# Feed-forward columns in five chunks of 128, and the last 42 of value and gate in one product

## The chip, the cores and the metric

The kernel runs on one NeuronCore of a Trainium2 chip. TensorE (PE; its weight loads are listed as PEld) multiplies, VectorE (DVE), ScalarE (ACT) and GpSimd (POOL) work element by element, SyncE (SP) issues most DMAs. The metric is the device time of one execution in microseconds (us), the median of several. All data are float32.

## What is computed

The reference is a stack: a chunked retention layer, two layers of local attention with a gated feed-forward, a latent attention, and a mixture of experts. The change touches the feed-forward of the two local-attention layers:

```python
DIM = 256
DEPTH = 2
HID = int(DIM * 4 * 2 / 3)          # 682
...
h = shift_token(x)
mu = h.mean(-1, keepdims=True)
var = h.var(-1, keepdims=True)
h = (h - mu) / jnp.sqrt(var + 1e-05) * lg + lb
h = h @ w1 + b1                      # w1: 256 x 1364
a, g = jnp.split(h, 2, axis=-1)      # value a and gate g, 682 columns each
h = a * jax.nn.gelu(g, approximate=False)
x = x + h @ w2 + b2
```

## The kernel before

The 4096 tokens go through in 8 pieces of 512. With two layers there are 16 items, k = 0 to 15, and the loop over `stages()` runs one stage for each: its feed-forward, beside the attention of the next item (`s.ahead`), and in stages 0 to 7 the retention layer (`s.ret`), in stages 8 to 15 the latent attention of a finished piece (`s.lat`, `s.behind`). Stage 15 is the last and has no next item. After it come 71 tiles of the experts. Each engine has its own program and the order in it is written out by hand; the engines meet at semaphores: `mmA` and `mmD` count finished products of PE, `outA` (ACT), `outS` and `outD` (DVE) count results that were read out of PSUM.

PSUM is two rings of four banks. Ring A (`pA`) is read mainly by ACT, ring D (`pD`) by DVE. `ring_a_jobs()` and `ring_d_jobs()` list the products in order; `bank_ring` gives each one or two banks (two start at an even bank, so that one may be left empty ahead of them) and works out which reader has to be done before PE may write there.

The feed-forward of one item, transposed (columns of `w1` on the partitions, the 512 tokens along the row), runs in `NHC` = 6 chunks of `HCH` = 120 inner columns, the last of 82:

- PE, `up_projection(b, c)`: the gate ("g", ring A), then the value ("a", ring D), each 2 matmuls of 512 columns over 256 inputs (`project`, L703). The profile records each float32 matmul twice, so that a product is 4 records.
- ACT, `gelu(b, c)` (L1252): the gate with its bias out of ring A to `gl`.
- DVE, `gate_up(b, c)` (L1674): (value + bias) x gelu to `hT[c]`. Before the last chunk a memset (L1673) puts ones below its 82 rows, and the row of ones carries the bias `b2`.
- PE, `down_projection(b)` (L703 from `hT` and `w2` to `pD`): 24 matmuls, behind a wait for the last `gate_up`.

After the last chunk PE does, in stages 0 to 8, the first two score products of the next item, S0 and S1 (`local_scores`, L753), and then the down-projection. In stages 9 to 14 two groups of transposes of the latent attention stand ahead of S0 (`turn_attention`, L714), which ACT copies to `curT` (L1278) after the last gelu. In stage 15 a `latent_values` product (L870) stands there, and no scores. ACT goes on with the exponentials (L1209), for which it first loads another table; DVE with the row maxima of S0 (L1634).

Of the kernel before, what the change touches and what calls it, by code (L numbers as in the profile page):

```python
# [26 lines left out]
HCH = 120  # L27
NHC = 6
HSZ = [min(HCH, HID - HCH * c) for c in range(NHC)]

# [61 lines left out]
def ring_a_jobs():  # L92
# [3 lines left out]
    for s in stages():  # L96
# [22 lines left out]
        for c in range(NHC):  # L119
            if s.here:  # L120
                j += [("g", k, c)]
            if s.ahead and c == 0:
                j += [("qkT", k + 1, 1)]
            if s.last and c == 1:
                j += [("av", b - 1, 2)]
            if s.behind and c == (5 if s.last else 3):
                j += [("av", b - 1, 3)]
            if s.ret and 1 <= c < 5:
                j += [("rT", k, c - 1)]
            if s.behind and c == 5 and not s.last:  # L130
                j += [("attnT", b - 1, 0), ("attnT", b - 1, 1)]
            if s.ahead and c == 3:
                j += [("qkT", k + 1, 2)]
            if s.ahead and c == 4:
                j += [("qkT", k + 1, 3)]
# [124 lines left out]
def stream_layers(nc, I, x_d, S, out_d):  # L260
# [17 lines left out]
    with ctx:  # L278
# [7 lines left out]
        by_layer = (("wqkv", [P, DC, 3 * INNER]), ("wo", [P, 4, D]), ("ln", [P, 2, DC]), ("w1", [P, DC, 2 * HID]),  # L286
# [196 lines left out]
        norm_x = sem("norm_x")  # L483
        fin_silu = sem("fin_silu")
# [41 lines left out]
        def _(sp):  # L526
# [23 lines left out]
            for s in stages():  # L550
# [34 lines left out]
                if k == B - 1:  # L585
                    sp.wait_ge(outA, doneA["g", k, NHC - 1])
# [75 lines left out]
        def _(pe):  # L662
# [126 lines left out]
            def up_projection(b, c):  # L789
                n = HSZ[c]  # L790
                if c == 0:
                    pe.wait_ge(outA, doneA["zT", b, 1])
                ps = slotA("g", b, c)
                project(ps[0:n, 0:T], lambda k: W["w1"][:, k, HID + c * HCH:HID + c * HCH + n], lambda k: zT[:, k, :], DC).then_inc(mmA, 1)
                ps = slotD("a", b, c)
                project(ps[0:n, 0:T], lambda k: W["w1"][:, k, c * HCH:c * HCH + n], lambda k: zT[:, k, :], DC).then_inc(mmD, 1)
# [364 lines left out]
        def _(act):  # L1161
# [85 lines left out]
            def gelu(b, c):  # L1247
                n = HSZ[c]
                ps = takeA("g", b, c)
                if b > 0 or c >= 2:  # L1250
                    act.wait_ge(outD, doneD["a", b, c - 2] if c >= 2 else doneD["a", b - 1, NHC - 1])
                nc.scalar.activation(gl_of(b)[c % 2][0:n], ps[0:n, 0:T], ACT.Gelu, bias=W["b1"][0:n, 1, c:c + 1]).then_inc(outA, 1)  # L1252
# [312 lines left out]
        def _(dve):  # L1565
# [102 lines left out]
            def gate_up(b, c):  # L1668
                n = HSZ[c]
                ps = take("a", b, c)  # L1670
                dve.wait_ge(outA, doneA["g", b, c])
                if c == NHC - 1:
                    step(nc.vector.memset(hT_of(b)[NHC - 1][64:HCH], 1.0))  # L1673
# [473 lines left out]
def arrange(a):  # L2147
# [13 lines left out]
    r["w_w1"] = np.stack([ch(w) for w in a["L0_ffn_w1"]], 1)  # L2161
    b1 = np.zeros((HCH, DEPTH, 2, NHC), np.float32)
    w2 = np.zeros((HCH, DEPTH, NHC, D), np.float32)
    for l in range(DEPTH):
        for c in range(NHC):
            n = HSZ[c]
            for i in range(2):
                b1[0:n, l, i, c] = a["L0_ffn_b1"][l, i * HID + c * HCH:i * HID + c * HCH + n]
# [46 lines left out]
```

## Time and profile before

| | |
|---|---|
| median of 3 runs | 3048.02 us (3040.27 to 3054.22) |
| the profiled execution | 3047.79 us, its span 3045.9 us |
| PE busy | 2770.7 us, 91% of the span |
| DVE, ACT, POOL busy | 53%, 40%, 35% |
| the chain that ended last | PE 73%, DVE 12%, issue 4%, DMA 4%, POOL 3%, ACT 3% |
| mean granted TensorE clock | 0.963 of full speed |

A timeline row is: start, us, engine, line, operation, what is written from what, shapes, number of records, and in brackets how long the engine was idle before it and who released it. A group row gives, after the number of records, busy us and mean ns of one record, and the idle time in front. PE's records overlap: in a row of matmuls the next starts before the modelled end of the one ahead, so that spacing is read from starts. A stage lasts about 137 us up to stage 6 and 157 to 163 us from stage 9.

### The profile page before, as it was taken

What the parts mean: (1) busy time and instruction counts of PE and PEld (TensorE: products, weight loads), DVE (VectorE), ACT (ScalarE), POOL (GpSimd) and SP (SyncE); (2) the same over time, 40 slices, a digit from 0 to 9 for tenths busy, and PEclk for the clock granted to TensorE, in tenths of its full rate; (3) what the DMA queues carried; (4) which work ended last, traced back from release to release, by engine and by line L of the source; (5) the groups of instructions that cost most, each with busy time, mean ns of one, the idle gap of its engine ahead of it and who ended that gap; (6) DMA issues with size and microseconds to landing.
All of it is one profiled execution on the core that took longest, in us unless ns stands there. A gap on an engine that the chain in (4) does not pass through costs nothing.

```text
span 3045.9 us, 42333 instructions
## 1 busy us (share of the span) xinstructions
PE 2770.7 (91%) x15646; PEld 1863.9 (61%) x15646; DVE 1627.9 (53%) x3890; ACT 1213.3 (40%) x2265; POOL 1077.0 (35%) x767
## 2 busy tenths in 40 slices
PE   6999999999999899999989898999988899999992
PEld 3565656556565656555555555555554488999992
DVE  6656566575656456676676768585754520000003
ACT  4444444535344444444444544444543232222221
POOL 5423243343423233353444535353532321111113
PEclk8999999999999999999999999999998799999996
DMA  3000000000001011001010101010000367999886
GB/s 134 11 23 17 25 28 25 15 25 15 25 22 46 25 40 59 20 5 49 4 49 4 49 4 42 11 39 15 29 15 31 132 233 268 343 357 344 326 325 206
DMA packets 85767, 261.72 MB, mean 86 GB/s; under 512 B 10653, under 2 KB 49901, under 8 KB 66877
## 3 DMA queue, kind: packets, MB, share of 16 engines
q1 hardware_dynamic: 79084, 241.25, 21.9%
q0 software_dynamic: 6480, 17.77, 1.5%
q8 instruction: 128, 2.10, 0.3%
q14 instruction: 75, 0.61, 0.1%
HBM read 210.68 MB, written 44.11 MB: 84 GB/s over the span
## 4 chain that ended last, share of the span: by engine, by line
PE 73%; DVE 12%; issue 4%; DMA 4%; POOL 3%; ACT 3%; SPq 1%; POOLq 0%; DVEq 0%; ACTq 0%
PE s_pD L703 20%; PE s_pA L703 17%; PE s_pD L1155 7%; PE s_pA L1140 6%; PE s_pD L860 3%; PE s_pA L753 3%; PE s_pD L775 3%; PE s_pA L762 3%; DMA s_w_w<-rows_s 3%; DVE s_pairs L1735 2%; PE s_pA L742 2%; DVE s_qk L1634 2%; PE s_pA L870 2%; ACT s_qk L1209 1%; PE s_pD L941 1%
## 5 line engine op out<-in xcount | busy, mean ns | idle before, releaser
L1456 POOL TENSOR_TENSOR s_qk<-s_qk,s_rrec 128x1024 f32<-128x1024 f32 (+1 forms) x128 | 215.7, 1685 | 578.0 <-DVE s_rrec L1640 577.9
L1209 ACT ACTIVATE s_qk<-s_qk,s_mx 128x256 f32<-128x256 f32 (+1 forms) x512 | 239.9, 469 | 341.0 <-DVE s_mx L1634 340.3
L703 PE MATMUL s_pA<-s_w_wqkv,s_curT 128*128 128x512 f32 x768 | 354.3, 601 | 5.6 <-ACT s_curT L1185 3.7
L703 PEld LDWEIGHTS s_pA<-s_w_wqkv,s_curT 128*128 128x128 f32 x768 | 142.4, 191 | 176.6 <-issue 163.1
L1735 DVE TENSOR_SCALAR s_pairs<-s_pD 128x1024 f32<-128x1024 f32 (+1 forms) x192 | 194.4, 1038 | 103.9 <-PE s_pD L860 101.1
L2086 DVE COPY s_w_wo<-s_pD 128x256 f32<-128x256 f32 x71 | 30.0, 423 | 409.6 <-PE s_pD L1126 409.6
L1555 POOL DMA_INDIRECT acc_s<-s_w_w,s_sq x71 | 68.3, 962 | 458.9 <-ACT s_w_w L1397 451.6
L1450 POOL TENSOR_TENSOR s_rinv<-s_ssq,s_half 128x16 f32<-128x16 f32 x64 | 207.5, 3242 | 5.1
L860 PE MATMUL s_pD<-s_mixer 32*128 32x512 f32 (+3 forms) x1024 | 186.4, 477 | 23.6 <-DVE s_pairs L1735 18.5
L1446 POOL TENSOR_TENSOR s_qk<-s_qk,s_rot 128x1024 f32<-128x1024 f32 x64 | 150.5, 2351 | 135.5 <-DVE s_qk L1617 135.4
L703 PE MATMUL s_pA<-s_zT,s_w_w 128*120 128x512 f32 (+1 forms) x384 | 186.7, 609 | 1.1 <-ACT s_zT L1225 1.1
L1634 DVE CUSTOM_DVE_ANT_0 s_qk<-s_pA,s_maskw 128x256 f32<-128x256 f32 (+1 forms) x512 | 167.9, 385 | 31.2 <-PE s_pA L753 30.7
L1270 ACT ACTIVATE s_pairs<-s_pairs 128x2560 f32<-128x2560 f32 x64 | 149.7, 2338 | 87.3 <-DVE s_pairs L1735 87.2
L703 PE MATMUL s_pD<-s_zT,s_w_w 128*120 128x512 f32 (+1 forms) x384 | 181.7, 596 | 0.0
L860 PEld LDWEIGHTS s_pD<-s_mixer 32*128 32x128 f32 x1024 | 91.6, 193 | 130.6 <-issue 84.4
L1414 POOL TENSOR_TENSOR s_rs<-s_ve,s_half 128x4 f32<-128x4 f32 x40 | 41.1, 1026 | 363.9 <-DVE s_ve L1596 363.9
L762 PE MATMUL s_pA<-s_ident,s_qk 128*128 128x128 f32 x896 | 129.8, 287 | 40.3 <-issue 23.7
L753 PE MATMUL s_pA<-s_qkT 64*128 64x256 f32 (+1 forms) x1024 | 131.7, 380 | 29.9 <-DVE s_mx L1634 14.7
L1191 ACT COPY s_qk<-s_pA 128x1024 f32<-128x1024 f32 x64 | 64.6, 1010 | 217.2 <-PE s_pA L703 217.2
L762 PEld LDWEIGHTS s_pA<-s_ident,s_qk 128*128 128x128 f32 x896 | 99.2, 144 | 83.8 <-issue 58.1
L703 PEld LDWEIGHTS s_pD<-s_zT,s_w_w 128*120 128x120 f32 (+1 forms) x384 | 69.1, 180 | 98.6 <-issue 97.9
L1397 ACT ACTIVATE s_w_w<-s_pD,s_w_w 128x256 f32<-128x256 f32 x71 | 33.6, 473 | 236.8 <-PE s_pD L1155 236.8
(276 smaller groups left out, 5922.9 us busy)
## 6 DMA issues: line engine op xcount, KB each, us to landing
s_qkT<-in_m_w SPq DMA_DIRECT2D x48, 1024.0 KB, 5.2
s_v_tm<-in_m_w SPq DMA_DIRECT2D x24, 1024.0 KB
s_rot<-in_m_w SPq DMA_DIRECT2D x24, 1024.0 KB, 5.1
s_w_wqkv<-in_m_w SPq DMA_DIRECT2D x23, 1024.0 KB
s_qk<-in_m_w SPq DMA_DIRECT2D x23, 1024.0 KB, 6.1
s_w_w<-rows_s SPq DMA_DIRECT2D x71, 129.0 KB
s_cur<-in_x SPq DMA_DIRECT2D x8, 512.0 KB, 3.5
xn_s<-s_cur SPq DMA_DIRECT2D x8, 512.0 KB, 2.8
```

The lines of the kernel that those rows point to most:

```text
L703: last = nc.tensor.matmul(out, lhs(c), rhs(c), start=(c == 0), stop=(c == n - 1))
L753: last = nc.tensor.matmul(ps[:, place(i) * 256 + lo * P:(place(i) + 1) * 256], qkT[r, h // 2, tile_cols(t)], qkT[r, 4 + h // 2, (t - 1 + l ...
L762: last = nc.tensor.transpose(ps[:, (2 * i + k) * P:(2 * i + k + 1) * P], prob[w % 3][:, i * 256 + k * P:i * 256 + (k + 1) * P], ident[:])
L860: last = nc.tensor.matmul(ps[:, 512 * i + col:512 * i + col + T - kt * P], KT[rows, g % 2, tile_cols(kt)], QT[rows, g % 2, kt * P:T], star ...
L1140: last = nc.tensor.matmul(m_ph[u % 2][:, f * P:(f + 1) * P], m_w1[u % NW][:, c * F + f * P:c * F + (f + 1) * P], m_xT[:, u % 2, c * P:(c + ...
L1155: last = nc.tensor.matmul(m_py(w), m_hT[w % 2][:, f * P:(f + 1) * P], m_w2[w % NW][:, f * D:(f + 1) * D], start=(f == 0), stop=(f == FC - 1))
L1209: last = nc.scalar.activation(pi, pi, ACT.Exp, scale=-1.0, bias=mx[:, u, i:i + 1], accum_out=rsum[:, u, i:i + 1])
L1446: nc.gpsimd.tensor_tensor(qk[:, t, :], qk[:, t, :], rot[:, t % 2, :], ALU.add)
L1450: nc.gpsimd.tensor_tensor(rinv[:, t, :], ssq[:, t, :], half[:], ALU.pow).then_inc(rinv_rdy, 1)
L1456: nc.gpsimd.tensor_tensor(pi, pi, rrec[:, u, :].unsqueeze(2).broadcast_to((P, 4, 256 - lo)), ALU.mult).then_inc(p_rdy, 1)
L1634: last = nc.vector.tensor_tensor_reduce(out=prob[u % 3][:, h], in0=ps[:, h], in1=maskw[:, lo:256], scale=-1.0, scalar=3e38, op0=ALU.add, o ...
L1735: nc.vector.tensor_scalar(Pl[:, w % SLOTS, :, ROUND_AT[r]:ROUND_AT[r] + ROUND_N[r]], ps[:, :, 0:ROUND_N[r]], 80.0, -80.0, ALU.min, ALU.max ...
```

## The change

`HCH` becomes 128: five chunks of 128 inner columns and a last one of 42. The columns of `w1` are laid out in the order in which they are used: for each chunk its values, then its gates, and for the last chunk 42 values, 22 columns of zeros and 42 gates (`LAST_G` = 64). The last chunk is one product of 106 rows in ring D. ACT reads its gelu from rows 64 to 105 of that bank and counts it on a semaphore of its own, `last_gelu`; DVE waits for that, sets the ones in rows 32 to 63 of `hT[5]`, and reads the values from rows 0 to 41 of the same bank. The last gate leaves ring A's list.

```diff
-HCH = 120
+HCH = 128
 NHC = 6
 HSZ = [min(HCH, HID - HCH * c) for c in range(NHC)]
+LAST_G = 64
+UPW = 2 * HCH * (NHC - 1) + LAST_G + HSZ[-1]
...
         for c in range(NHC):
-            if s.here:
+            if s.here and c < NHC - 1:
                 j += [("g", k, c)]
...
                 if k == B - 1:
-                    sp.wait_ge(outA, doneA["g", k, NHC - 1])
+                    sp.wait_ge(outA, doneA["g", k, NHC - 2])
...
             def up_projection(b, c):
-                n = HSZ[c]
                 if c == 0:
                     pe.wait_ge(outA, doneA["zT", b, 1])
-                ps = slotA("g", b, c)
-                project(ps[0:n, 0:T], lambda k: W["w1"][:, k, HID + c * HCH:HID + c * HCH + n], lambda k: zT[:, k, :], DC).then_inc(mmA, 1)
+                at = 2 * HCH * c
+                if c < NHC - 1:
+                    ps = slotA("g", b, c)
+                    project(ps, lambda k: W["w1"][:, k, at + HCH:at + 2 * HCH], lambda k: zT[:, k, :], DC).then_inc(mmA, 1)
+                n = HCH if c < NHC - 1 else LAST_G + HSZ[c]
                 ps = slotD("a", b, c)
-                project(ps[0:n, 0:T], lambda k: W["w1"][:, k, c * HCH:c * HCH + n], lambda k: zT[:, k, :], DC).then_inc(mmD, 1)
+                project(ps[0:n, 0:T], lambda k: W["w1"][:, k, at:at + n], lambda k: zT[:, k, :], DC).then_inc(mmD, 1)
...
             def gelu(b, c):
                 n = HSZ[c]
-                ps = takeA("g", b, c)
+                at = 0 if c < NHC - 1 else LAST_G
+                if c < NHC - 1:
+                    ps = takeA("g", b, c)
+                else:
+                    act.wait_ge(mmD, DJ["a", b, c] + 1)
+                    ps = pD[:, colsD[DJ["a", b, c]]]
                 if b > 0 or c >= 2:
                     act.wait_ge(outD, doneD["a", b, c - 2] if c >= 2 else doneD["a", b - 1, NHC - 1])
-                nc.scalar.activation(gl_of(b)[c % 2][0:n], ps[0:n, 0:T], ACT.Gelu, bias=W["b1"][0:n, 1, c:c + 1]).then_inc(outA, 1)
+                last = nc.scalar.activation(gl_of(b)[c % 2][0:n], ps[at:at + n, 0:T], ACT.Gelu, bias=W["b1"][at:at + n, 1, c:c + 1])
+                last.then_inc(outA if c < NHC - 1 else last_gelu, 1)
...
             def gate_up(b, c):
                 n = HSZ[c]
                 ps = take("a", b, c)
-                dve.wait_ge(outA, doneA["g", b, c])
-                if c == NHC - 1:
-                    step(nc.vector.memset(hT_of(b)[NHC - 1][64:HCH], 1.0))
+                if c < NHC - 1:
+                    dve.wait_ge(outA, doneA["g", b, c])
+                else:
+                    dve.wait_ge(last_gelu, b + 1)
+                    step(nc.vector.memset(hT_of(b)[NHC - 1][32:64], 1.0))
```

PE in stage 0, from the last transposes of the up-projection to the down-projection, before (`s_zT,s_w_w` are the up-projection, `s_qkT` the scores S0 and S1, `s_w_w,s_pairs` the down-projection):

```order
L742 MATMUL s_pA<-s_ident,s_qk 128x128 x7
L703 MATMUL s_pA<-s_zT,s_w_w 82x512 [waits s_outS,s_outA]
L703 MATMUL s_pA<-s_zT,s_w_w 82x512
L703 MATMUL s_pD<-s_zT,s_w_w 82x512 [waits s_outD]
L703 MATMUL s_pD<-s_zT,s_w_w 82x512
L753 MATMUL s_pA<-s_qkT 128x128 [waits s_outS,s_outA]
L753 MATMUL s_pA<-s_qkT 128x128 x3
L753 MATMUL s_pA<-s_qkT 128x128 [waits s_outS,s_outA]
L753 MATMUL s_pA<-s_qkT 128x128 x3
L703 MATMUL s_pD<-s_w_w,s_pairs 128x256 [waits s_outD,s_down_in]
```

The same stretch of PE in the changed kernel:

```order
L745 MATMUL s_pA<-s_ident,s_qk 128x128 x7
L706 MATMUL s_pD<-s_zT,s_w_w 106x512 [waits s_outD]
L706 MATMUL s_pD<-s_zT,s_w_w 106x512
L756 MATMUL s_pA<-s_qkT 128x128 [waits s_outS,s_outA]
L756 MATMUL s_pA<-s_qkT 128x128 x3
L756 MATMUL s_pA<-s_qkT 128x128 [waits s_outS,s_outA]
L756 MATMUL s_pA<-s_qkT 128x128 x3
L706 MATMUL s_pD<-s_w_w,s_pairs 128x256 [waits s_outD,s_down_in]
```

Two matmuls are gone; what stands between the last product and the down-projection is the same.

ACT at the same place in stage 9, before (`s_curT` are the transposes of the latent attention):

```order
L1202 COPY s_qkT<-s_pA 128x8x128 [waits s_mmA]
L1252 ACTIVATE s_pairs<-s_pA,s_w_b 82x512 [waits s_outD,s_mmA]
L1278 COPY s_curT<-s_pA 128x2x256 [waits s_mmA] x2
L1209 ACT_TABLE_LOAD
L1209 ACTIVATE s_qk,s_rsum<-s_qk,s_mx 128x128 [waits s_outS]
```

ACT there in the changed kernel:

```order
L1207 COPY s_qkT<-s_pA 128x8x128 [waits s_mmA]
L1262 ACTIVATE s_pairs<-s_pD,s_w_b 42x512 [waits s_outD,s_mmD]
L1289 COPY s_curT<-s_pA 128x2x256 [waits s_mmA] x2
L1214 ACT_TABLE_LOAD
L1214 ACTIVATE s_qk,s_rsum<-s_qk,s_mx 128x128 [waits s_outS]
```

The order on ACT is the same; the last gelu now waits for a product of ring D. On DVE the memset waited for `outA` and `mmD` and now waits for `last_gelu` and `mmD`:

```order
L1686 MEMSET s_pairs 32x512 [waits s_last_gelu,s_mmD]
L1687 SCALAR_TENSOR_TENSOR s_pairs<-s_pD,s_w_b,s_pairs 42x512 [waits s_v_step]
L1645 ISA s_qk,s_mx<-s_pA,s_maskw 128x128 [waits s_mmA]
```

Behind it stand, as before, the product that writes `hT[5]` and the row maxima of S0.

## Rows read from the trace of the kernel before

**Rows 1.** The page, busy us of each engine.

```profile
PE 2770.7 (91%) x15646; PEld 1863.9 (61%) x15646; DVE 1627.9 (53%) x3890; ACT 1213.3 (40%) x2265; POOL 1077.0 (35%) x767
```

**Rows 2.** Groups of instructions by form: up-projection, retention products, down-projection, weight loads.

```profile
L703 PE MATMUL s_pD<-s_mixer 128*128 128x512 f32 x128 | 60.2, 592 | 0.0
...
L703 PE MATMUL s_pA<-s_zT,s_w_w 128*82 128x512 f32 x64 | 30.1, 592 | 0.0
...
L703 PE MATMUL s_pD<-s_w_w,s_pairs 120*128 120x256 f32 x360 | 89.0, 383 | 3.7 <-DVE s_pairs L1674 2.8 <-issue 0.9
...
L703 PE MATMUL s_pD<-s_w_w,s_pairs 83*128 83x256 f32 x120 | 35.8, 379 | 0.0
...
L703 PEld LDWEIGHTS s_pA<-s_zT,s_w_w 128*120 128x120 f32 x320 | 55.4, 189 | 52.0 <-issue 50.4 <-ACT s_zT L1225 1.5
```

**Rows 3.** Timeline of stage 3, PE, ACT and DVE around its last chunk.

```profile
571.53 1.88 PE L703 MATMUL s_pA<-s_zT,s_w_w 128*82 128x512 f32 x4
...
573.25 1.88 PE L703 MATMUL s_pD<-s_zT,s_w_w 128*82 128x512 f32 x4
...
573.45 0.68 ACT L1252 ACTIVATE s_pairs<-s_pA,s_w_b 82x512 f32<-82x512 f32 x1 [0.71 <-PE s_pA L703]
...
574.15 1.28 ACT L1209 ACT_TABLE_LOAD   x1
...
575.06 1.16 PE L753 MATMUL s_pA<-s_qkT 64*128 64x128 f32 x16
575.30 0.48 DVE L1673 MEMSET s_pairs<- 56x512 f32 x1 [2.49 <-PE s_pD L703]
575.82 0.75 DVE L1674 SCALAR_TENSOR_TENSOR s_pairs<-s_pD,s_w_b,s_pairs 82x512 f32<-82x512 f32 x1
...
576.62 1.56 PE L703 MATMUL s_pD<-s_w_w,s_pairs 120*128 120x256 f32 x6 [0.40 <-DVE s_pairs L1674]
...
577.44 0.40 ACT L1209 ACTIVATE s_qk<-s_qk,s_mx 128x128 f32<-128x128 f32 x1 [2.01 <-DVE s_mx L1634]
```

**Rows 4.** Timeline of stage 10, PE and ACT after the last gate.

```profile
1561.50 1.88 PE L703 MATMUL s_pD<-s_zT,s_w_w 128*82 128x512 f32 x4
1561.70 0.68 ACT L1252 ACTIVATE s_pairs<-s_pA,s_w_b 82x512 f32<-82x512 f32 x1 [0.70 <-PE s_pA L703]
...
1563.22 1.04 PE L714 MATMUL s_pA<-s_ident,s_mixer 128*128 128x128 f32 x8
...
1563.86 1.07 ACT L1278 COPY s_curT<-s_pA 128x512 f32<-128x512 f32 x2 [1.47 <-PE s_pA L714]
...
1564.54 1.20 PE L753 MATMUL s_pA<-s_qkT 64*128 64x128 f32 x16 [0.29 <-ACT s_curT L1278]
...
1565.67 1.56 PE L703 MATMUL s_pD<-s_w_w,s_pairs 120*128 120x256 f32 x6
```

**Rows 5.** Timeline of stage 15, the last chunk and what follows.

```profile
2339.85 1.88 PE L703 MATMUL s_pD<-s_zT,s_w_w 128*82 128x512 f32 x4
...
2342.27 0.68 ACT L1252 ACTIVATE s_qkT<-s_pA,s_w_b 82x512 f32<-82x512 f32 x1
...
2343.19 0.48 DVE L1673 MEMSET s_qkT<- 56x512 f32 x1 [4.04 <-ACT s_qkT L1252]
...
2343.72 3.34 PE L870 MATMUL s_pA<-s_pairs,s_mixer 128*32 128x512 f32 x32 [1.98 <-POOL s_pairs L1469]
```

**Rows 6.** Timeline of PE: a wait in stage 3, and stage 15's first product.

```profile
612.68 1.14 PE L753 MATMUL s_pA<-s_qkT 64*128 64x256 f32 x8 [1.41 <-ACT s_PT_even L1219]
...
2308.13 3.77 PE L703 MATMUL s_pA<-s_zT,s_w_w 128*120 128x512 f32 x4 [1.11 <-ACT s_zT L1225]
```

**Rows 7.** Stretches: length, busy PE, PEld, DVE, ACT, POOL, granted clock, DMA share, GB/s.

```profile
610.50:619.70 9.20, 7.12 (x72) 5.64 (x70) 7.61 (x27) 6.07 (x19) 5.05 (x4) 1.00 0.00 0
...
2302.00:2309.00 7.00, 3.10 (x9) 1.91 (x10) 3.85 (x8) 3.73 (x6) 2.83 (x3) 0.50 0.01 2
```

More of the change, by code:

```diff
@@ L285, in stream_layers @@
         W = {}
-        by_layer = (("wqkv", [P, DC, 3 * INNER]), ("wo", [P, 4, D]), ("ln", [P, 2, DC]), ("w1", [P, DC, 2 * HID]),
+        by_layer = (("wqkv", [P, DC, 3 * INNER]), ("wo", [P, 4, D]), ("ln", [P, 2, DC]), ("w1", [P, DC, UPW]),
                     ("b1", [HCH, 2, NHC]), ("w2", [HCH, NHC, D]), ("qks", [P, 2, 2, DH]))
@@ L483, in stream_layers @@
         norm_x = sem("norm_x")
+        last_gelu = sem("last_gelu")
         fin_silu = sem("fin_silu")
@@ L2160, in arrange @@
     r["w_ln"] = np.stack([np.stack([per(g), per(b)], 1) for g, b in zip(a["L0_ffn_ln_g"], a["L0_ffn_ln_b"])], 1)
-    r["w_w1"] = np.stack([ch(w) for w in a["L0_ffn_w1"]], 1)
+    up = []
+    for c in range(NHC):
+        value = a["L0_ffn_w1"][:, :, c * HCH:c * HCH + HSZ[c]]
+        gate = a["L0_ffn_w1"][:, :, HID + c * HCH:HID + c * HCH + HSZ[c]]
+        room = np.zeros(value.shape[:2] + (LAST_G - HSZ[c] if c == NHC - 1 else 0,), np.float32)
+        up += [value, room, gate]
+    r["w_w1"] = np.stack([ch(w) for w in np.concatenate(up, 2)], 1)
     b1 = np.zeros((HCH, DEPTH, 2, NHC), np.float32)
@@ L2167, in arrange @@
             for i in range(2):
-                b1[0:n, l, i, c] = a["L0_ffn_b1"][l, i * HID + c * HCH:i * HID + c * HCH + n]
+                at = LAST_G if i and c == NHC - 1 else 0
+                b1[at:at + n, l, i, c] = a["L0_ffn_b1"][l, i * HID + c * HCH:i * HID + c * HCH + n]
             w2[0:n, l, c] = a["L0_ffn_w2"][l, c * HCH:c * HCH + n]
```

## The prediction

> **What bounds the kernel now.** I read the page first, then the groups of instructions, then the timeline around the last chunk of each of the 16 items. The page has PE busy for 2770.7 of 3045.9 us, against 1627.9 for DVE and less for ACT [rows 1]: PE's stream is the time, save where it waits. So the question is where PE gets work taken away and whether it then only waits for what used to finish behind that work. At the last chunk of stage 3 the reader is to see a row of products without gaps, the gate at 571.53 and the value at 573.25, the scores S0 and S1 at 575.06, and then PE idle for 0.40 us ahead of the down-projection at 576.62, released by DVE's product L1674 [rows 3]. That place is already a wait on the chain value, memset, L1674. In the group row the releases by L1674 sum to 2.8 us, seven times 0.4 (stages 1 to 7), and the 0.9 put down to issue are stages 0 and 8, 0.45 each [rows 2]: nine stages of 16 have the wait. Stages 9 to 14 have none there, but a 0.29 ahead of S0, for ACT's copy of the transposes [rows 4]. Stage 15 waits 1.98 for GpSimd's masks [rows 5].
>
> **What is removed.** One product of two matmuls for each item, 4 records, 64 in all [rows 2]. The gate of stage 3 takes from 571.53 to 573.25, 1.72 us of PE's stream [rows 3]. 16 x 1.72 = 27.5 us gross.
>
> **What is widened.** Ten products per item go from 120 to 128 rows, the combined one has 106. A record of 82 rows and one of 128 both take a mean 592 ns [rows 2], so the widths between them cost nothing more. The down-projection contracts over 128 or 43 rows instead of 120 or 83; its records take 383 and 379 [rows 2]: zero as well. ACT's and DVE's work goes along the 512 tokens, and the shapes differ only in partitions: zero, with other work in front of it anyway. The load of `w1` grows by 44 columns in 2728, 1.6%; its second copy is started in stage 7 and used in stage 8, so it is covered, and so is the first, issued at the start and used after more than 100 us.
>
> A weight load of 120 columns takes 189 ns beside records that start every 430 ns, and the load engine's idle time is put down to issue, not the other way round [rows 2]. That speaks for zero. The Trainium skill ("TensorE: Matmul & The Clock Gate", LDWEIGHTS) says that a load takes as long as it has columns, at 1.2 per ns; by it 8 more columns in 640 loads would be 4.3 us, an estimate, if none of it were hidden. The trace has the loads hidden.
>
> **What is added: a serial gelu.** Before, ACT's gelu of the gate ran beside the value product. Now it starts only when the one product ends. That product stands in the gate's old slot and ends at the same time, so ACT starts at 573.45 in stage 3's clock, as before; it had been idle for 0.71 us [rows 3], so nothing holds it up. Then DVE. How long it takes from the start of the last gelu to the memset when ACT releases it shows in stage 15: 2342.27 to 2343.19, 0.92 us [rows 5]. Memset to L1674 is 575.30 to 575.82, 0.52; L1674 to the down-projection is 575.82 to 576.62, 0.80 [rows 3]. The sum is 2.24 us, so the down-projection starts at 573.45 + 2.24 = 575.69 instead of 576.62. **Gain 0.93 us**, not 1.72: S0 and S1 now end near 574.5, and PE's wait grows from 0.40 to about 1.2 us. Nine such stages give 8.4 us. DVE had been idle 2.49 us ahead of the memset [rows 3], so it's there in time. Behind the memset on DVE wait the row maxima of S0, which come 0.93 earlier too. ACT's table load ends at 575.43, and the first exponential would start at 577.44 - 0.93 = 576.51 [rows 3]: covered by 1.1 us, and if it weren't, the down-projection of some 10 us covers the rest.
>
> **Stages 9 to 14.** Stage 10 stands for the six. The combined product takes the slot that ends at 1561.50, the gelu starts at 1561.70 as before, and the copies of the transposes can follow it. In stage 3 the next ACT instruction starts 0.70 after the gelu's start [rows 3], so the copies start at 1562.40 instead of 1563.86. From their start to the down-projection it was 1.81 us [rows 4], and I keep that, since S1 needs the second copy: 1564.21. The gate chain would allow 1561.70 + 2.24 = 1563.94, which is earlier. So the copies decide, and the gain is 1565.67 - 1564.21 = **1.46 us**, 8.8 us for six. S0 no longer waits for the first copy, because the ring lost an odd job and its slot lies elsewhere; the wait moves to S1. No other slot in ring A waits for a later reader than before. The bounds of this term are 0.93 (if it behaved as stage 3) and 1.72.
>
> **Stage 15.** L870 starts when GpSimd releases it at 2343.72, and the last gelu came at 2342.27, after an exponential [rows 5]. Neither depends on the product removed. Gain 0; PE's idle time there grows from 1.98 to some 3.7 us.
>
> **Is it kept?** After the down-projection's start all engines are shifted alike: the rest of a stage begins with that product, and what comes from memory for it is started by events that shift with it. Sum 8.4 + 8.8 + 0 = 17.2 us. Against the profiled execution's own 3047.79 that is 3030.6; the median of the three runs is 0.2 higher, so 3030.8.
>
> **Rivals.**
>
> *The wait does not show (full gain).* If PE never waited for the last `gate_up`, all 27.5 us would come: 3020.5. The 0.40 already there speaks against it: the chain to the down-projection gets longer after the product, not shorter. It would need DVE's answer to be 0.8 us quicker than its rows.
>
> *The latent stages give nothing.* In stages 9 to 14 DVE and GpSimd carry the router's small steps and the scatter of rows between the last chunk and the scores. If one of those, tied to an earlier point of the stage, is what ends last, the 8.8 us are taken back further on, and 8.4 are left: 3048.0 - 8.4 = 3039.6. For it: DVE's sequence right behind the last `gate_up` waits for a scatter. Against it: the down-projection, some 10 us of PE, lies between that and the next thing that PE needs from DVE.
>
> *Slower: the clock.* The granted clock was 0.50, the 1.2 GHz level, from 2302 to 2309 [rows 7], where PE was busy for 3.10 of 7 us, and the next product took 3.77 for 4 records, against 1.88 at the full 2.4 GHz [rows 3, 6]: 1.89 us more. My nine waits of 1.2 us could bring such drops where there are none. If one product's worth of work in each of 15 stages ran at the low level, that is 15 x 1.89 = 28.4 us, more than the 17.2: 3030.8 + 28.4 = 3059.2. It decides from 17.2 / 1.89, some 9 products' worth. Against it: PE waited 1.41 us at 612.68 and the stretch around it kept a clock of 1.00 with PE busy for 7.12 of 9.20 us [rows 6, 7]; after the last chunk PE is far busier than that. The Trainium skill ("TensorE: Matmul & The Clock Gate", What's actually happening) has the clock follow how busy the array has been lately, with the low level as its rest. By that rule longer waits can only move things toward the low level; the row at 612.68 says that one of this length in busy surroundings doesn't.
>
> *It doesn't do what it says.* The two matmuls are gone from PE's order, so this is left with next to nothing.
>
> **How the numbers follow.** My forecast has 0.62, the latent stages giving nothing 0.20, the full gain 0.10, the clock 0.06, anything else 0.02. A measurement of this kernel can tell about 0.5%, 15.2 us, from no change, so the line is at 3032.8. The forecast lies 2 us beyond it, and a median of runs that spread from 3040 to 3054 moves by some 3 us: of its 0.62 I count 0.48 as faster and 0.14 as same. With the full gain faster comes to 0.58; with the latent rival same comes to 0.34 and, with a share of the clock case that stays under the line, 0.36; slower 0.06. The range goes from the full gain, 3020, to the latent rival with 2 us of spread, 3042.
>
> **What will show it.** Idle ahead of the down-projection in stages 0 to 8: 1.2 us, released by L1687 or issue (0.4 would mean the full gain). Start of the last gelu to the down-projection: 2.24 us. S0 without a wait in stages 9 to 14, one of about 0.6 for the copies between S0 and S1, and the down-projection 4.4 us after the start of the combined product instead of 5.9 after that of the gate. Stage 15's L870 at the same distance from its fourth gelu as before. A distance between equal points of stages 2 and 3 of some 137 - 0.9 us. I'd be wrong if the six latent stages didn't get shorter by 1.5 us each, if the clock of stages 0 to 8 fell below 1.00, or if the records of the combined product or of the 128-row products took longer than the 592 ns of before.

## The result

The changed kernel takes 3056.34 us, median of 20 runs (3051.73 to 3071.3), against 3047.9 us for the kernel before beside it. The ratio is 1.0039, with a 95% interval from 1.0027 to 1.0050: slower by some 8 us, where I had forecast 3030.8 and a range from 3020 to 3042. The profiled execution took 3053.22 us, its span 3051.2.

The page of the changed kernel, busy time of the engines:

```profile
PE 2768.3 (91%) x15582; PEld 1858.8 (61%) x15582; DVE 1634.7 (54%) x3890; ACT 1214.7 (40%) x2265; POOL 1078.4 (35%) x767
```

64 records of PE are gone, which at 592 ns less their overlap are 27.5 us, yet PE's busy time is only 2.4 us lower than in [rows 1]. Something on PE has become dearer. The groups of PE show what (busy us, mean ns of one record | idle time ahead):

```profile
L706 PE MATMUL s_pD<-s_w_w,s_pairs 128*128 128x256 f32 x360 | 93.7, 397 | 10.7 <-DVE s_pairs L1687 8.2 <-issue 2.4
L706 PE MATMUL s_pD<-s_w_w,s_pairs 43*128 43x256 f32 x120 | 41.8, 428 | 0.0
L706 PE MATMUL s_pD<-s_zT,s_w_w 128*106 128x512 f32 x64 | 30.1, 592 | 0.0
```

The combined product of 106 rows costs 592 ns a record, as the products before did. The down-projection doesn't: its last chunk went from 379 to 428 ns a record and the chunks beside it from 383 to 397 [rows 2]. Stage 3 of the changed kernel, to be laid beside [rows 3]:

```profile
574.01 1.88 PE L706 MATMUL s_pD<-s_zT,s_w_w 128*106 128x512 f32 x4
575.82 1.16 PE L756 MATMUL s_pA<-s_qkT 64*128 64x128 f32 x16
...
575.93 0.68 ACT L1262 ACTIVATE s_pairs<-s_pD,s_w_b 42x512 f32<-42x512 f32 x1 [0.71 <-PE s_pD L706]
576.84 0.48 DVE L1686 MEMSET s_pairs<- 32x512 f32 x1 [1.55 <-ACT s_pairs L1262]
577.37 0.74 DVE L1687 SCALAR_TENSOR_TENSOR s_pairs<-s_pD,s_w_b,s_pairs 42x512 f32<-42x512 f32 x1
...
578.16 1.56 PE L706 MATMUL s_pD<-s_w_w,s_pairs 128*128 128x256 f32 x6 [1.18 <-DVE s_pairs L1687]
579.56 1.03 PE L706 MATMUL s_pD<-s_w_w,s_PT_even 128*128 128x256 f32 x4
580.52 2.19 PE L706 MATMUL s_pD<-s_w_w,s_pairs 43*128 43x256 f32 x8
582.54 1.03 PE L706 MATMUL s_pD<-s_w_w,s_PT_even 128*128 128x256 f32 x4
```

Up to 578.16 this is the prediction: 2.23 us from the gelu to the down-projection, a wait of 1.18. Behind it the row of eight records that begins with the 43-row product takes 2.02 us from start to start, and the row ahead of it 0.96. The same two rows of the kernel before:

```profile
578.02 1.03 PE L703 MATMUL s_pD<-s_w_w,s_PT_even 120*128 120x256 f32 x4
578.88 1.89 PE L703 MATMUL s_pD<-s_w_w,s_pairs 83*128 83x256 f32 x8
580.62 1.03 PE L703 MATMUL s_pD<-s_w_w,s_PT_even 120*128 120x256 f32 x4
```

There they took 0.86 and 1.74 us. A quarter of the down-projection (12 records) went from 2.60 to 2.98 us. The weight loads, first of before, then of the changed kernel, say where in it:

```profile
578.67 1.71 PEld L703 LDWEIGHTS s_pD<-s_w_w,s_pairs 83*128 83x128 f32 x8
```

```profile
580.52 0.29 PEld L706 LDWEIGHTS s_pD<-s_w_w,s_pairs 43*128 43x128 f32 x2 [0.33 <-issue]
581.14 1.16 PEld L706 LDWEIGHTS s_pD<-s_w_w,s_pairs 128*128 128x128 f32 x6 [0.33 <-issue]
```

Before, the loads of a row began 0.21 us ahead of its matmuls (578.67 and 578.88) and ran on without a gap. Now the load of the 43-row weights begins together with its matmul, at 580.52, after 0.33 us without a load, and the first load of 128 rows behind it has the same gap.

The first transposes behind the down-projection (PT0), of before and of the changed kernel:

```profile
588.26 0.66 PE L762 MATMUL s_pA<-s_ident,s_qk 128*128 128x128 f32 x4
```

```profile
590.96 0.66 PE L765 MATMUL s_pA<-s_ident,s_qk 128*128 128x128 f32 x4
```

Over an item, from the start of the down-projection to PT0, it was 588.26 - 576.62 = 11.64 us and is 590.96 - 578.16 = 12.80: **1.16 us more**, 18.6 us for 16 items, against the 17.2 that I had counted as gain.

The distance between equal points of two stages (the memset of the last chunk) puts both together. Undisturbed, it was 136.85 us in the retention stages and is 137.2; in the latent ones 156.8 and 156.6. With nine of the former and six of the latter that is 9 x 0.35 - 6 x 0.2 = 2 us, and 3 with the down-projection of stage 15: not yet 8. The rest shows where stages are disturbed. In the profiled runs three of the first six distances of the changed kernel came to 138.8 or 138.9 us, at a clock of 0.99, against one of 138.4 in the kernel before. These falls are at one place in both kernels, behind an old wait for ACT some 38 us after the memset, and none is at the wait that the change makes longer. Stage 1 of the kernel before, and stage 0 of the changed one:

```profile
337.42 1.64 PE L753 MATMUL s_pA<-s_qkT 64*128 64x256 f32 x8 [1.41 <-ACT s_PT_even L1219]
```

```profile
200.63 1.98 PE L756 MATMUL s_pA<-s_qkT 64*128 64x256 f32 x8 [1.40 <-ACT s_PT_even L1224]
```

The same wait in stage 3 of the kernel before had no fall, and the products behind it took 1.14 us [rows 6]. Further on, from the memset of stage 9 to that of stage 14, with the length of each, busy PE, PEld, DVE, ACT, POOL, and the granted clock; before:

```profile
1401.70:1563.50 161.80, 148.59 (x826) 88.61 (x824) 111.43 (x250) 73.45 (x127) 74.15 (x54) 0.96 0.07 25
1563.50:1720.40 156.90, 142.54 (x827) 84.50 (x826) 111.12 (x251) 73.45 (x127) 74.33 (x54) 1.00 0.08 26
1720.40:1877.20 156.80, 142.44 (x826) 84.42 (x825) 111.04 (x250) 73.45 (x127) 74.31 (x54) 1.00 0.08 26
1877.20:2034.00 156.80, 142.43 (x826) 84.42 (x825) 111.04 (x250) 73.46 (x127) 74.31 (x54) 1.00 0.07 26
2034.00:2196.90 162.90, 151.30 (x827) 89.84 (x826) 111.81 (x251) 73.45 (x127) 74.11 (x54) 0.94 0.07 25
```

and the changed kernel, the third and the fourth of these stages:

```profile
1721.90:1886.20 164.30, 152.73 (x822) 91.70 (x822) 112.05 (x250) 73.39 (x128) 74.06 (x55) 0.93 0.07 25
1886.20:2042.80 156.60, 142.11 (x822) 83.90 (x824) 111.68 (x250) 73.46 (x128) 74.31 (x55) 1.00 0.08 26
```

The kernel before has three stages in a row of 156.8 us at a clock of 1.00. In the changed one a stage of the same work, 156.6 us long when undisturbed, comes to 164.3 at 0.93. Over its 20 runs the mean granted clock is 0.961, against 0.965 for the kernel before in its runs beside the experiments; of its runs beside this result only the profiled one's clock is on record, 0.963. So there were two suspects, a product of 43 rows among ones of 128, and the clock.

### The profile page after: what moved, and what is told of

Read it like the earlier page. It is cut to its first block, busy times and chain, and to the rows that moved or that the text cites. A ratio compares the mean times of both kernels' runs of the same rounds, so it can differ in the third digit from the quotient of the medians.

```text
span 3051.2 us, 42189 instructions
## 1 busy us (share of the span) xinstructions
PE 2768.3 (91%) x15582; PEld 1858.8 (61%) x15582; DVE 1634.7 (54%) x3890; ACT 1214.7 (40%) x2265; POOL 1078.4 (35%) x767
## 4 chain that ended last, share of the span: by engine, by line
PE 72%; DVE 12%; issue 4%; DMA 4%; ACT 3%; POOL 3%; SPq 1%; POOLq 0%; DVEq 0%; ACTq 0%
PE s_pD L706 21%; PE s_pA L706 16%; PE s_pD L1160 7%; PE s_pA L1145 6%; PE s_pD L865 3%; PE s_pD L778 3%; PE s_pA L756 3%; PE s_pA L765 3%; DMA s_w_w<-rows_s 3%; DVE s_pairs L1748 2%; PE s_pA L745 2%; DVE s_qk L1645 2%; PE s_pA L875 2%; ACT s_qk L1214 1%; PE s_pD L946 1%
## 5 line engine op out<-in xcount | busy, mean ns | idle before, releaser
L706 PE MATMUL s_pD<-s_zT,s_w_w 128*128 128x512 f32 (+1 forms) x384 | 180.8, 594 | 0.0
L756 PE MATMUL s_pA<-s_qkT 64*128 64x256 f32 (+1 forms) x1024 | 142.2, 387 | 32.7 <-DVE s_mx L1645 15.9
L706 PE MATMUL s_pA<-s_zT,s_w_w 128*128 128x512 f32 x320 | 155.6, 610 | 1.1 <-ACT s_zT L1230 1.1
L706 PE MATMUL s_pD<-s_w_w,s_pairs 128*128 128x256 f32 x480 | 132.3, 405 | 10.7 <-DVE s_pairs L1687 8.2
L756 PEld LDWEIGHTS s_pA<-s_qkT 64*128 64x128 f32 x1024 | 95.5, 195 | 62.0 <-issue 24.4
```

The source lines that it names most:

```text
L706: last = nc.tensor.matmul(out, lhs(c), rhs(c), start=(c == 0), stop=(c == n - 1))
L756: last = nc.tensor.matmul(ps[:, place(i) * 256 + lo * P:(place(i) + 1) * 256], qkT[r, h // 2, tile_cols(t)], qkT[r, 4 + h // 2, (t - 1 + l ...
```

## The experiments

Retention stage is the distance between two memsets at a granted clock of 1.00; latent five is the distance from stage 9 to stage 14 in the profiled run; the clock is the mean over all runs (for the kernel before, over its runs beside the experiments). The kernel before ran beside each group, at 3044.6 (e1, e2, e3, e6), 3045.9 (e4, e5, e8, e9) and 3046.5 us (the last four), with a clock of 0.965 each time. So medians of different groups can be some 3 us apart for the same kernel.

| kernel | median us | ratio to before, 95% | clock | retention stage | latent five |
|---|---|---|---|---|---|
| before | 3047.9 | | 0.965 | 136.85 | 795.2 |
| changed | 3056.3 | 1.0027 to 1.0050 | 0.961 | 137.2 | 800.6 |
| e1_k128 | 3052.7 | 1.0021 to 1.0047 | 0.957 | 136.1 | 801.7 |
| e2_k64 | 3066.9 | 1.0070 to 1.0098 | 0.959 | 137.2 | 802.1 |
| e3_before43 | 3076.1 | 1.0095 to 1.0124 | 0.964 | 138.0 | 805.6 |
| e6_alternate | 3059.5 | 1.0032 to 1.0068 | 0.959 | 136.85 | 807.0 |
| e4_apart | 3073.7 | 1.0072 to 1.0107 | 0.966 | 138.1 | 809.0 |
| e5_k65 | 3043.8 | 0.9987 to 1.0017 | 0.959 | 136.1 | 802.0 |
| e8_late_wait | 3042.5 | 0.9967 to 0.9997 | 0.956 | 134.8 | 807.8 |
| e9_k128_pad | 3038.8 | 0.9964 to 0.9986 | 0.965 | 136.1 | 798.6 |
| e10_late_pad3 | 3030.1 | 0.9928 to 0.9961 | 0.963 | 134.8 | 799.8 |
| e12_late_pad5 | 3046.8 | 0.9991 to 1.0023 | 0.959 | 134.8 | 812.2 |
| e11_before_less | 3051.9 | 1.0005 to 1.0031 | 0.959 | 136.85 | 802.4 |
| e13_before_pad | 3054.6 | 1.0017 to 1.0038 | 0.967 | 136.85 | 802.0 |

### How many rows the last contraction has

**e1_k128**, the last contraction over 128 rows:

```diff
-                rows = [min(HCH, HSZ[c] + (c == NHC - 1)) for c in range(NHC)]
+                rows = [HCH] * (NHC - 1) + [HCH]
...
+                    step(nc.vector.memset(hT_of(b)[NHC - 1][64:HCH], 1.0))
```

> The changed kernel, but the last chunk of the down-projection contracts over 128 rows instead of 43 (the rows of w2 behind the 43 are zeros; hT gets ones there by one more memset ahead of the wait for the last gelu). Theory T, that going between a contraction of 128 rows and one of 43 stops PE: the eight breaks per item go, a quarter of the down-projection takes 2.60 us again instead of 2.98, the first PT0 starts about 11.6 us after the down-projection instead of 12.80, and with 16 items the kernel is 19 to 24 us faster than the changed one, about 3035 us. Rival R1, that the product of 43 rows is itself slow, whatever stands beside it: about the same gain, so this run doesn't part T and R1. Rival R2, that the loss comes from the granted clock or from the wait for the serial gelu: within 3 us of the changed kernel, 3056 us.

**e2_k64**, the same with `[64]` and without the memset:

> The changed kernel with a contraction of 64 rows in the last chunk of the down-projection instead of 43 (the rows of w2 behind the 43 are zeros). If what matters is that the 43 rows are an odd or uneven count (R1), this run gains like the one of 128 rows, about 20 us, to some 3035 us. If 64 rows are still of the same small kind as 43 (T), nothing changes: within 3 us of the changed kernel, a quarter stays at 2.98 us.

**e5_k65**, the same with `[65]`, with the memset:

> The last contraction over 65 rows, one more than in e2_k64, with the memset of e1_k128. If going between contractions costs only up to 64 rows, this runs as e1_k128 does: a quarter of the down-projection in 2.60 us, retention stages of 136.1 us, 3050 to 3055 us. If the cost came of any contraction shorter than its neighbours, and grew with the difference, it would be nearer to e2_k64: 2.98 us and 137.2 us, 3062 us or more.

The rows of the last chunk in the down-projection, in e1 (where all chunks are one group), e2 and e5:

```profile
L706 PE MATMUL s_pD<-s_w_w,s_pairs 128*128 128x256 f32 x480 | 117.3, 382 | 10.7 <-DVE s_pairs L1688 8.2 <-issue 2.4
```

```profile
L706 PE MATMUL s_pD<-s_w_w,s_pairs 64*128 64x256 f32 x120 | 41.8, 428 | 0.0
```

```profile
L706 PE MATMUL s_pD<-s_w_w,s_pairs 65*128 65x256 f32 x120 | 35.8, 379 | 0.0
```

64 rows cost what 43 cost, 428 ns; 65 rows cost 379, as 83 did, and in e1 128 rows cost 382 with all chunks together. It isn't the number of rows by degrees, and not an odd count: the step lies between 64 and 65. The quarter of the down-projection is back to 2.60 us in e1 and e5, and the retention stage to 136.1 us, 0.75 under the kernel before. The time of e2, 3066.9 us, missed both expectations: it is 10 us above the changed kernel with the same stage of 137.2 us.

The time in e1 isn't what was expected: 3052.65, not 3035. In the stages the gain is there; it is lost elsewhere, at a clock of 0.957, the lowest so far. e5 has the same order of work and the same stage lengths, and came to 3043.8. In its own runs the time follows the clock: the fastest, 3036.13 us, had 0.963, the slowest, 3056.93 us, 0.956. So this group settles the first suspect and points to the second. But it also shows a third source of difference: behind the memset of stage 15, where no edit reaches and the work is the same in all kernels, the profiled runs took from 697.3 us (e5) to 715.2 us (e10). Of the 9.3 us between the profiled runs of e1 and e5, 6.4 stand there, and of the 9.6 between those of e2 and the changed kernel 6.7. What moves it is open.

**e3_before43**, the kernel before with the last contraction cut to 43 rows:

```diff
-                rows = [min(HCH, HSZ[c] + (c == NHC - 1)) for c in range(NHC)]
+                rows = [HCH] * (NHC - 1) + [43]
```

> The kernel before with one number changed: the last chunk of its down-projection contracts over 43 rows instead of 83. It leaves out the inner columns behind the 43rd of the last chunk and the row that carries b2; no product is taken away. Everything else, the serial gelu and the order included, is the kernel before. T: the eight breaks per item come in, 16 x 1.2 to 1.5 us = 19 to 24 us on top of the kernel before, 3067 to 3072 us, and a quarter takes 2.98 us instead of 2.60. R2: no change, within 3 us of the kernel before.

One number in the kernel before does it: the last chunk's records take 428 ns, the quarter 2.98 us, and the retention stage goes from 136.85 to 138.0 us. 16 x 1.15 = 18 us is what the profiled run lost (3066.18 against 3047.79). The median is 31 us above the kernel beside it, at nearly its clock; the 13 us between 18 and 31 I can't place.

**e4_apart**, the changed kernel with the last value and gate as two products again:

```diff
-                if c < NHC - 1:
-                    ps = slotA("g", b, c)
-                    project(ps, lambda k: W["w1"][:, k, at + HCH:at + 2 * HCH], lambda k: zT[:, k, :], DC).then_inc(mmA, 1)
-                n = HCH if c < NHC - 1 else LAST_G + HSZ[c]
+                n = HSZ[c]
+                off = HCH if c < NHC - 1 else LAST_G
+                ps = slotA("g", b, c)
+                project(ps[0:n], lambda k: W["w1"][:, k, at + off:at + off + n], lambda k: zT[:, k, :], DC).then_inc(mmA, 1)
```

> Chunks of 128 with the last 42 values and 42 gates as two products, as in the kernel before; the gelu of the last chunk runs beside the value's product again. The contraction of the last chunk is 43 rows. By theory T the combined product is not what costs, and this kernel pays the breaks at 43 rows in full with nothing to set against them: retention stages of 138.0 us, as in the kernel before with 43 rows, the whole 18 to 30 us slower than the kernel before, 3063 to 3075 us. By R2 (the serial gelu is the loss) it is as fast as the kernel before, 3045 us.

As T had it: 138.1 us a stage and 28 us over the kernel before. So the chunks of 128, by the remainder of 42 that they leave, are what costs, and the combined product earns: the changed kernel is 0.9 us a stage and 17 us in all (3073.7 - 3056.3) faster than this one. The serial gelu (R2) is not the loss.

**e6_alternate**, the chunks of every second token tile in reverse:

```diff
-                        last = project(ps[:, k * D:(k + 1) * D], lambda c: hT_of(b)[c][0:rows[c], tile_cols(2 * i + k)], lambda c: W["w2"][0:rows[c], c, :], NHC)
+                        turn = (lambda c: c) if k == 0 else (lambda c: NHC - 1 - c)
+                        last = project(ps[:, k * D:(k + 1) * D], lambda c: hT_of(b)[turn(c)][0:rows[turn(c)], tile_cols(2 * i + k)], lambda c: W["w2"][0:rows[turn(c)], turn(c), :], NHC)
```

> The changed kernel with the chunks of every second token tile taken in reverse order, so that the last chunks of two token tiles stand side by side: two rows of 43-row products meet, and of eight changes between 128 and 43 rows per item four are left. The number of products and of weight loads is the same. T: half of the loss goes, 9 to 12 us faster than the changed kernel, 3044 to 3047 us. R1 (the 43-row product is slow in itself) and R2 (clock or gelu): nothing goes, within 3 us of 3056 us.

The same products in another order: two 43-row blocks now meet, and two quarters take 583.82 - 578.25 = 5.57 us where they took 2 x 2.98 = 5.96:

```profile
578.25 1.13 PE L706 MATMUL s_pD<-s_w_w,s_pairs 43*128 43x256 f32 x4
579.31 1.13 PE L706 MATMUL s_pD<-s_w_w,s_PT_even 128*128 128x256 f32 x4
580.28 2.75 PE L706 MATMUL s_pD<-s_w_w,s_pairs 128*128 128x256 f32 x12
582.87 1.03 PE L706 MATMUL s_pD<-s_w_w,s_PT_even 128*128 128x256 f32 x4
583.82 1.13 PE L706 MATMUL s_pD<-s_w_w,s_pairs 43*128 43x256 f32 x4
```

So the price belongs to the change between kinds and not to the 43-row product: 0.38 us for a pair of changes, 0.19 each on average. The expectation counted eight changes an item, of which four would go. There were seven, because the next scores (S2) have 64 rows and followed the last 43-row records without a break (matmuls of both kinds start at 589.46 and 589.48). In e6 the down-projection ends with 128 rows, so five are left, two fewer, and the stage gained 0.38 (136.86 for 137.24), not 0.58. The kernel before has one change, from its 83 rows to S2; the six more of the changed kernel, at 0.19 each, are the 1.16 us of an item. In the whole time nothing of it shows; the latent five, 807.0, took it back. My expectation for the sum failed.

### The clock and the length of a stage

What decides where the clock falls? The length of a single idle time doesn't. PE waits 2.64 us for DVE at the same place in every latent stage. In stage 11 of the kernel before the clock stayed at 1.00 through it and behind it:

```profile
1691.36 0.63 PE L878 MATMUL s_pD<-s_ident,s_mixer 128*128 128x128 f32 x4 [2.64 <-DVE s_pairs L1735]
```

```profile
1690.00:1692.00 2.00, 0.64 (x6) 0.68 (x7) 2.00 (x3) 0.24 (x1) 2.00 (x3) 1.00 0.00 0
1692.00:1694.00 2.00, 2.00 (x12) 1.26 (x11) 1.97 (x5) 1.09 (x2) 2.00 (x2) 1.00 0.03 8
```

In stage 12 of the changed kernel it fell to the 1.2 GHz level, and the transposes took 1.09 us instead of 0.63:

```profile
1856.71 1.09 PE L883 MATMUL s_pD<-s_ident,s_mixer 128*128 128x128 f32 x4 [2.64 <-DVE s_pairs L1748]
```

```profile
1854.00:1856.00 2.00, 0.06 (x1) 0.00 (x0) 2.00 (x2) 1.59 (x4) 2.00 (x3) 1.00 0.00 0
1856.00:1858.00 2.00, 1.29 (x6) 1.32 (x7) 1.86 (x3) 0.00 (x0) 2.00 (x4) 0.56 0.00 0
1858.00:1860.00 2.00, 2.00 (x10) 1.72 (x9) 1.93 (x5) 0.46 (x1) 2.00 (x1) 0.59 0.00 0
```

The same idle time, the same work around it, two outcomes: what differs is when it comes. That fits a clock that looks at PE on a beat of its own. The Trainium skill ("TensorE: Matmul & The Clock Gate", What's actually happening) says this of it: the activity window is "free-running", and doesn't start with the kernel. If so, a stage whose length goes evenly into that beat meets it each time at the same moment, and three stages in a row without a fall are what a length of 156.8 us looks like. That is theory C. It can be tried by changing nothing but the length of the latent stages.

**e9_k128_pad**, e1 with 1.3 us of useless work in each of stages 9 to 14:

```diff
+                        if i == 0 and k == 0 and 9 <= b <= 14:
+                            for _ in range(3):
+                                nc.tensor.matmul(ps[:, 0:D], hT_of(b)[0][0:HCH, tile_cols(0)], W["w2"][0:HCH, 0, :], start=True, stop=True)
```

> The kernel with the last contraction over 128 rows (e1_k128), with three idle products of 256 columns set ahead of the down-projection in stages 9 to 14; they write where the down-projection then begins afresh, and each costs 0.43 us: 1.3 us per stage, 7.7 us in all. In e1_k128 the retention stages took 136.1 us against 136.85 before and those of the latent attention, falls of the clock taken out, 155.7 against 156.8; yet three of them in a row came to 160.4 to 162.4, each with 10 to 20 us at the low clock, where the kernel before has three of 156.8 with none. Theory C, that a stage whose length repeats at 156.8 to 157 us meets the clock's falls each time at the same, harmless moment, and one that repeats at 155.7 doesn't: with the stage brought back to 157.0 us the falls go from stages 10 to 12, they take 157 us again, and the kernel gets faster by doing more, 3036 to 3044 us against 3052.65. Rival D, that the lower clock comes with the denser work and not with when it comes, or from chance: the padding costs its 7.7 us, 3058 to 3062 us.

**e11_before_less**, the kernel before with 1.3 us of its work left out in the same stages:

```diff
+                        less = 3 if i == 0 and k == 0 and 9 <= b <= 14 else 0
-                        last = project(ps[:, k * D:(k + 1) * D], lambda c: hT_of(b)[c][0:rows[c], tile_cols(2 * i + k)], lambda c: W["w2"][0:rows[c], c, :], NHC)
+                        last = project(ps[:, k * D:(k + 1) * D], lambda c: hT_of(b)[c + less][0:rows[c + less], tile_cols(2 * i + k)], lambda c: W["w2"][0:rows[c + less], c + less, :], NHC - less)
```

> The kernel before with three of the 24 products of the down-projection left out in stages 9 to 14 (chunks 0 to 2 of the first token tile, so that their inner columns are missing there). Work of 3 x 0.43 = 1.3 us per stage goes, nothing is added, and no contraction is changed. D, each stage 1.3 us shorter and the clock as before: 7.7 us faster than the kernel before, 3038 us. C: a stage of 155.5 us doesn't repeat at the harmless moment; stages 10 to 12 come to 160 us or more with 10 us or more at the low clock, where the kernel before has 156.8 and none, the mean granted clock falls from 0.965 to 0.955 to 0.960, and the kernel with less work is as slow as the kernel before or slower, 3045 to 3056 us.

The kernel that does more than e1 is 14 us faster, 3038.8, clock 0.965 instead of 0.957. Against e5, which has the stage lengths of e1 and ran in the same group as e9 (3043.8, clock 0.959), it is 5 us faster; so the sign is firmer than the size. The kernel that does less than the kernel before is 5 us slower, 3051.9, clock 0.959. Its stages 10 to 12, where the kernel before has 156.8 at 1.00 (the second to the fourth row of its stretches above):

```profile
1561.10:1721.50 160.40, 147.55 (x820) 87.55 (x819) 111.70 (x250) 73.45 (x127) 74.12 (x54) 0.96 0.07 25
1721.50:1882.10 160.60, 147.33 (x821) 87.63 (x820) 111.25 (x251) 73.46 (x127) 74.15 (x54) 0.96 0.08 26
1882.10:2042.40 160.30, 147.42 (x820) 87.51 (x819) 111.79 (x250) 73.46 (x127) 74.11 (x54) 0.96 0.07 25
```

1.3 us of work went and the stage got 3.6 us longer, three times alike: the falls bring it to another length, and that one repeats. A stage of e1 does the same:

```profile
1716.90:1877.30 160.40, 145.35 (x822) 87.33 (x824) 113.38 (x251) 73.42 (x128) 74.07 (x55) 0.97 0.08 26
1877.30:2037.70 160.40, 145.49 (x822) 87.46 (x824) 113.27 (x251) 73.48 (x128) 74.14 (x55) 0.97 0.07 25
```

**e13_before_pad**, the kernel before with the three useless products:

> The kernel before with the three idle products of e9_k128_pad ahead of the down-projection in stages 9 to 14, which makes a latent stage 158.1 us, as long as those of e4_apart (clock 0.966) and of e3_before43 (0.964). D: 7.7 us slower than the kernel before, 3054 us. C: the stages are longer than those that repeat, yet e3_before43 and e4_apart show no lower clock at this length, so by what the runs show so far 7.7 us as well, 3052 to 3058 us, clock 0.963 to 0.966. If the same three products gain 14 us in e9_k128_pad and lose 8 here, their own effect on the engine isn't what matters.

Here the same products cost: 3054.6, 8 us over the kernel before, at a clock of 0.967. Padding isn't good in itself.

**e8_late_wait**, both memsets ahead of the wait, and PE's wait moved behind five chunks:

```diff
-                pe.wait_ge(outD, doneD["a", b, NHC - 1])
+                pe.wait_ge(outD, doneD["a", b, NHC - 2])
...
+                        for c in range(NHC):
+                            if c == NHC - 1 and i == 0 and k == 0:
+                                pe.wait_ge(outD, doneD["a", b, NHC - 1])
+                            last = nc.tensor.matmul(out, hT_of(b)[c][0:rows[c], tile_cols(2 * i + k)], W["w2"][0:rows[c], c, :], start=(c == 0), stop=(c == NHC - 1))
...
+                    nc.vector.memset(hT_of(b)[NHC - 1][64:HCH], 1.0)
+                    nc.vector.memset(hT_of(b)[NHC - 1][32:64], 1.0)
                     dve.wait_ge(last_gelu, b + 1)
```

> The last contraction over 128 rows, both memsets set ahead of the wait for the last gelu, and PE's wait for the last gate_up moved from the head of the down-projection to the first product that reads it, the sixth. The chain gelu, gate_up, down-projection is then covered by five chunks, 2.2 us. Against e1_k128 the idle 1.2 us ahead of the down-projection goes in stages 0 to 8: retention stages of 134.9 to 135.1 us against 136.1. In the latent stages, where the wait isn't what decides, nothing changes, 155.7 us. By the chain alone 9 x 1.1 = 10 us less than e1_k128, 3043 us; by theory C the latent stages keep their falls of the clock (10 us at the low clock or more in each of stages 10 to 12) and 3043 stands, within 5 us.

The wait is gone and the retention stage is 134.8 us, 2.0 under the kernel before. Its latent five take 807.8, 12.6 more than in the kernel before, though a latent stage has less to do: clock 0.956, the time 3042.5.

**e10_late_pad3** and **e12_late_pad5**, e8 with three and with five useless products:

```diff
+                        if i == 0 and k == 0 and 9 <= b <= 14:
+                            for _ in range(3):
+                                nc.tensor.matmul(out, hT_of(b)[0][0:HCH, tile_cols(0)], W["w2"][0:HCH, 0, :], start=True, stop=True)
```

> e8_late_wait with three idle products ahead of the down-projection in stages 9 to 14. The retention stages of e8_late_wait are 134.8 us against 136.1 of e1_k128; its latent stages come to 157.1 to 163.9 us at a clock of 0.955. C: with the stage brought to some 156.6 to 157.0 us the clock comes back to 0.962 to 0.966, and the gain of the retention stages, 9 x 1.3 = 12 us on e9_k128_pad's 3038.8, stands: 3027 to 3033 us. D: 7.7 us slower than e8_late_wait, 3050 us.

> As e10_late_pad3 with five idle products, 2.15 us per stage. C: if a stage a little too long does no harm (e4_apart, e3_before43), the clock is that of e10_late_pad3 and the time 6 x 0.86 = 5.2 us above it, 3032 to 3038 us; if the length has to be met closely, the clock falls again and the time is over 3040 us. D: 3055 us.

With three products the time is 3030.1 us, 12 under e8 and 0.6% under the kernel before, the best of all; two of its latent stages:

```profile
1545.10:1701.80 156.70, 142.21 (x828) 85.36 (x826) 111.63 (x251) 73.46 (x128) 74.33 (x55) 1.00 0.08 26
...
1858.60:2023.00 164.40, 152.79 (x827) 93.31 (x826) 111.94 (x251) 73.39 (x128) 74.06 (x55) 0.93 0.07 25
```

With five, in the same group, the clock is 0.959 and the time 3046.8, 17 us more for two products: the second reading that C left open, a length that has to be met closely. The two also say what C doesn't explain. Even with three products a stage of 164.4 stands among those of 156.7, and e13, whose undisturbed stage of 158.1 us is longer than e12's (some 157.6, an estimate from e10's 156.7 and two products of 0.43), has the best clock of all. So shown is that 1.3 us more or less in a latent stage, with nothing else changed, moved the mean clock by 0.006 to 0.008 in three pairs of four (e1 and e9, e8 and e10, before and e11; not before and e13), and there the time against the work. Of these only the pairs with the kernel before ran in one group. That this comes by the moments at which PE's idle times fall is the reading that fits; it is argued, not shown, and I can't forecast from it which length is good.

## Why the prediction was wrong

**The step that failed first** is under "What is widened": "The down-projection contracts over 128 or 43 rows instead of 120 or 83; its records take 383 and 379: zero as well". Two groups, both over 64 rows, carried a statement on 43. The term was 1.16 us per item, 18.6 us, and ate the whole gain. The trace of before could have told: the first load for the scores S0, 64 rows behind products of 128, begins at 575.06 with the matmul itself and after 0.80 us without a load, where others lead:

```profile
575.06 0.97 PEld L753 LDWEIGHTS s_pA<-s_qkT 64*128 64x128 f32 x16 [0.80 <-issue]
```

The Trainium skill ("TensorEngine Tiling (Array Packing)", Key Properties) says that "Changing tiling mode (not just tile) drains the TensorE", and its list of configurations has row tiles of 64. The step between 64 and 65 rows and the 0.19 us for a change agree with that, if a contraction of at most 64 rows is run as such a tile, which no run shows; the page names no price. I had not looked there, since the change asks for no tiling.

**The step that failed second** is "Is it kept?": "After the down-projection's start all engines are shifted alike ... Sum 8.4 + 8.8 + 0 = 17.2 us". With the first fault mended (e1, e5) the retention stages gained 0.75 of the 0.93 forecast, and yet the kernel came to 3052.7 and 3043.8 instead of some 3031. Not all engines are shifted alike: PE's wait for ACT's copy ahead of a later score product grew by 0.14 us in a retention stage, from before to e1 (and to 0.38 in the changed kernel too):

```profile
592.52 1.13 PE L753 MATMUL s_pA<-s_qkT 64*128 64x256 f32 x8 [0.24 <-ACT s_PT_even L1219]
```

```profile
590.39 1.14 PE L756 MATMUL s_pA<-s_qkT 64*128 64x256 f32 x8 [0.38 <-ACT s_PT_even L1224]
```

And the shift isn't neutral for the clock, as the runs with padding argue. My rival had the clock, at 0.06, but by another mechanism: nine waits of 1.2 us in stages 0 to 8. In the profiled run the clock fell at none of those. It fell at waits that had always been there, most of them in the latent stages, three in stages 0, 2 and 5. What I held against the rival, the wait of 1.41 us at 612.68 at a clock of 1.00, was one stage's luck: behind the same wait at 337.42 the kernel before has a fall.

**What held.** The product removed is worth 1.72 us of PE's row, and the combined one costs 592 ns a record. The chain from the last gelu to the down-projection took 2.23 us (2.24), the wait 1.18 (1.2), released by L1687 in seven stages, and by issue in stages 0 and 8. In stage 15 PE's idle time is 3.69 us (3.7). In stage 10 the down-projection started 4.45 us after the combined product (4.4), with S0 free and a wait of 0.40 at S1 (some 0.6):

```profile
1562.48 1.88 PE L706 MATMUL s_pD<-s_zT,s_w_w 128*106 128x512 f32 x4
...
1566.28 0.71 PE L756 MATMUL s_pA<-s_qkT 64*128 64x128 f32 x8 [0.40 <-ACT s_curT L1289]
1566.93 0.92 PE L706 MATMUL s_pD<-s_w_w,s_pairs 128*128 128x256 f32 x3
```

So a term of +18.6 was missing from the sum, and one of 9 x 0.14 = 1.3, which makes 3051. The other 5 to 6 us stand beside a clock of 0.961 instead of 0.965. That they are the clock's is an estimate by the slope of e5's own runs (20.8 us for 0.007), which could carry more; the stretch behind stage 15, up to 18 us apart between profiled runs, is a rival that the medians can't part from it. The latent rival (3039.6) didn't come: those stages gained at the gate what was forecast and lost it in the down-projection, like the others.

## What to carry to other kernels

When chunks are cut anew, look at the last one: a remainder of 64 or fewer rows of contraction (43 and 64 were tried) among larger ones costs two changes each time it comes round, 0.38 us here, and filling it with rows of zeros to 65 or more costs nothing on PE. Cost an operation by a row of its own kind, and if there is none, look for the nearest place where the kinds already meet. Where a loop's stages repeat within a few hundredths of a microsecond and run at the full clock, a small gain in each can be lost to the clock; compare the granted clock over several runs beside the time, and try a few lengths before a good edit is thrown away.

## What the runs showed of the hardware

- The step in the cost of a contraction lies between 64 rows (428 ns a record) and 65 (379 ns), beside products of 128 rows and with equal columns; a change of kind costs 0.19 us on average, and none is paid between 43 and 64 rows.
- Leaving out 1.3 us of work in six of 16 stages made a kernel 5 us slower (interval 1.5 to 9 us), and adding as much made another faster, by 14 us against e1 and by 5 against e5. In both the latent stages' own undisturbed length was what the edit moved.
- The clock fell behind an idle time of 2.64 us in one stage and not in another with the same work around it, and likewise behind one of 1.4 us in the retention stages.
